# Cross-attention and quantised FFN on one core: setup work, the first and the last step put in another order, and Wo's low part moved to GpSimd

## The reference

```python
y_dca, y_main = y[:, -DCA:, :], y[:, :-DCA, :]
kv_dca = (y_dca @ Wkv_dca + bkv_dca).reshape(b, DCA, 2, H, HD)
k_dca = _ln(kv_dca[:, :, 0], kn_dca_w, kn_dca_b)
v_dca = kv_dca[:, :, 1]
q = _ln((x @ Wq + bq).reshape(b, s1, H, HD), qn_w, qn_b)
k = _ln(kv[..., :HD], kn_w, kn_b)          # kv from y_main @ Wk, y_main @ Wv
ctx = _attn(qT, k, v) + _attn(qT, k_dca, v_dca)
return ctx @ Wo + bo
...
x = x + xattn(_layernorm(x), ctx_1024, ...)
x = x + ffn(_layernorm(x), kernel, bias)   # fake_quant of x, kernel, bias and of relu(...)
```

## Time and profile before

| what | value |
|---|---|
| median of three runs | 357.25 us (355.57, 361.37, 357.25) |
| the profiled execution | 358.21 us, its span 356.4 us |
| PE busy | 326.6 us, 92% of the span |
| DVE busy | 314.6 us, 88% |
| ACT busy | 222.0 us, 62% |
| POOL busy | 173.9 us, 49% |
| shares of the chain that ended last | PE 60%, POOL 8%, DVE 5% |

### The profile page before, as it was taken

One profiled execution on the slowest core, in us unless ns is written; L12 is line 12 of the kernel. 1 busy time (PEld: TensorE's weight loads), 2 busy tenths in 40 slices (PEclk: granted clock), 3 DMA queues, 4 the chain that ended last, 5 costly groups with the idle time before them and its releaser, 6 DMA issues.

```text
span 356.4 us, 7623 instructions
## 1 busy us (share of the span) xinstructions
PE 326.6 (92%) x2372; PEld 257.8 (72%) x2372; DVE 314.6 (88%) x804; ACT 222.0 (62%) x444; POOL 173.9 (49%) x261
## 2 busy tenths in 40 slices
PE   6697879899999999999999999999999999987871
PEld 2354657778888878787878787878787878775640
DVE  2997998889989999999999999999999999986665
ACT  3357986356585858585858585858585856472401
POOL 6211613317282828282828383837373747372720
PEclk9999998699999999999999999999999999999895
DMA  7970334304241514242424242333333323230002
GB/s 259 272 286 3 103 111 151 115 14 136 49 148 48 175 50 149 76 159 67 151 76 147 77 137 90 125 103 118 109 120 106 121 63 120 63 125 25 30 1 88
DMA packets 36451, 38.88 MB, mean 109 GB/s; under 512 B 8760, under 2 KB 27452, under 8 KB 36412
## 3 DMA queue, kind: packets, MB, share of 16 engines
q1 hardware_dynamic: 36044, 38.14, 33.0%
q10 hardware_dynamic: 368, 0.27, 0.3%
HBM read 16.89 MB, written 4.72 MB: 61 GB/s over the span
## 4 chain that ended last, share of the span: by engine, by line
PE 60%; POOL 8%; DVE 5%; issue 4%; ACT 2%; DMA 1%; POOLq 0%; ACTq 0%; DVEq 0%
PE bank L1330 33%; PE bank L1453 9%; POOL finals L536 5%; PE bank L1433 3%; PE bank L1627 3%; PE bank L1434 3%; PE bank L1422 2%; PE bank L1617 2%; PE bank L1474 2%; PE bank L1507 2%; PE bank L1512 1%; POOL x_small L593 1%; DVE seg_out L1075 1%; ACT prob_store L750 1%; DVE rden L1069 1%
## 5 line engine op out<-in xcount | busy, mean ns | idle before, releaser
L517 POOL TENSOR_TENSOR k_lo<-wkv_raw,k_hi 128x448 f16<-128x448 f32 x16 | 16.8, 1047 | 110.5 <-issue 92.9
L1453 PE MATMUL bank<-v_aug,prob_store 128*128 128x66 f32 x512 | 67.9, 276 | 2.7 <-ACT prob_store L750 2.7
L1453 PEld LDWEIGHTS bank<-v_aug,prob_store 128*128 128x128 f32 x512 | 63.7, 193 | 5.2 <-ACT prob_store L750 4.0
L761 ACT ACTIVATE wkv_raw<-bank,affine 128x448 f32<-128x448 f32 (+1 forms) x32 | 22.6, 749 | 40.6 <-PE bank L1507 40.2
L1062 DVE TENSOR_REDUCE neg_max<-bank 128x4 f32<-128x448 f32 (+1 forms) x128 | 44.9, 412 | 0.3 <-PE bank L1422 0.3
L750 ACT ACTIVATE prob_store<-bank,exp_scale 128x512 f32<-128x512 f32 x64 | 41.6, 678 | 4.9 <-PE bank L1434 4.8
L536 POOL TENSOR_TENSOR finals<-seg_out 128x128 f32<-128x128 f32 x64 | 34.5, 547 | 12.5 <-DVE seg_out L1075 11.9
L1433 PE MATMUL bank<-q_stack,k_stack 128*128 128x128 f16 x256 | 33.9, 220 | 0.6 <-ACT maxT L612 0.6
L1434 PE MATMUL bank<-maxT,sel 128*128 128x128 bf16 x256 | 33.7, 219 | 0.0
L1075 DVE TENSOR_TENSOR seg_out<-bank,rden 128x256 f32<-128x256 f32 x64 | 27.2, 424 | 4.0 <-POOL finals L536 1.7
L1433 PEld LDWEIGHTS bank<-q_stack,k_stack 128*128 128x128 f16 x256 | 26.4, 104 | 5.2 <-issue 3.9
(11 more groups left out here) (213 smaller groups left out, 893.7 us busy)
## 6 DMA issues: line engine op xcount, KB each, us to landing
x_in<-in_x SPq DMA_DIRECT2D x16, 256.0 KB, 3.2
q_stack<-q_hi SPq DMA_DIRECT2D x32, 128.0 KB, 2.1
q_stack<-q_lo SPq DMA_DIRECT2D x32, 128.0 KB, 2.1
k_stack<-k_hi SPq DMA_DIRECT2D x32, 128.0 KB, 2.1
k_stack<-k_lo SPq DMA_DIRECT2D x32, 128.0 KB, 2.1
out<-finals SPq DMA_DIRECT2D x16, 256.0 KB, 2.0
y_dcaT<-in_x SPq DMA_DIRECT2D x8, 256.0 KB, 2.9
x_res<-in_x SPq DMA_DIRECT2D x8, 256.0 KB, 2.8
```

The source lines that it names most:

```text
L761: s.activation(n.rearrange("p (c n) -> p c n", n=P)[:, :, 0:keys], src, ACT.Identity, bias=shift, scale=gain).then_inc(n_ready.sem, 1)
L1453: last = mm(bank[6 + gr % 2][:, VW * h:VW * (h + 1)], probs[:, gr % 2, h], v_aug[:, Bt.parity, HG * gr + h], start=True, stop=True)
```

## The change

It has seven parts, none of which changes what is computed. (1) ScalarE copies the selectors in step -2, before the high part of Wq. (2) In step -2 VectorE adds the keys' bias (`biased_keys`) before `setup_norms`, and ScalarE squares the queries before `setup_heads` and `setup_columns`. (3) VectorE works on `setup_ffn(0)` before `low_query` in step 0. (4) `low_output` goes from VectorE to GpSimd, in four pieces of 512 columns between the DCA columns and k's low part of step 0. (5) `setup_ffn_bias` goes from the start of step 0 to the end of step 1, behind the sums of squares and ahead of the maxima. (6) Step 0 on TensorE gets the order of the other steps. (7) In the step where the last batch is Bt, TensorE makes three products of 512 columns (`turn_over`) behind `weigh(2)`, whose result nobody reads.

```diff
+            def low_output():
+                pool.wait_ge(wohi_ready.sem, 1)
+                for c in range(XC):
+                    ins = g.tensor_tensor(wo_lo[:, c], wo_raw[:, c], wo_hi[:, c].bitcast(FP32), ALU.subtract)
+                ins.then_inc(wolo_ready.sem, 1)
@@ pool, step @@
                         dca_columns(k_lo, kdca_lo)
+                        if N.second():
+                            low_output()
                         low(k_lo, k_n, k_hi, kn_ready, khi_ready, kstack_in, klo_ready, MAIN)
@@ scalar @@
                 setup_transposed()
+                setup_selectors()
                 for half in range(2):
@@ scalar, step @@
                         token_statistics()
+                        squared_queries()
+                        setup_heads()
                         setup_columns()
-                        setup_heads()
...
-                if A is not None:
-                    act.wait_ge(*qraw_ready.of(A))
-                    if A.has(1):
-                        act.wait_ge(*qss_ready.of(A.back(1)))
-                    s.activation(q_sq, q_raw[:, A.parity], ACT.Square).then_inc(qsq_ready.sem, 1)
+                if A is not None and not A.first():
+                    squared_queries()
                 if N is not None and N.first():
                     heads(A)
                     setup_wo()
                     setup_values()
                     setup_ffn()
-                    setup_selectors()
@@ vector @@
-            def low_output():
-                dve.wait_ge(wohi_ready.sem, 1)
-                v.tensor_tensor(wo_lo[:], wo_raw[:], wo_hi[:].bitcast(FP32), ALU.subtract).then_inc(wolo_ready.sem, 1)
@@ vector, step @@
-                if Bt is not None and Bt.first():
-                    setup_ffn_bias()
...
                     if A.first():
                         low_queries()
+                        biased_keys()
                         setup_norms()
                         setup_affine()
-                        biased_keys()
                         setup_squares()
                 if Bt is not None and Bt.first():
+                    setup_ffn(0)
                     low_query()
-                    low_output()
-                    setup_ffn(0)
...
                         head_products(A)
+                    if C is not None and C.first():
+                        setup_ffn_bias()
                     maxima(0)
                     maxima(1)
@@ tensor, step @@
-                if Bt is not None and not Bt.first():
+                if Bt is not None:
                     transposed_maxima()
...
-                if Bt is not None and Bt.first():
-                    transposed_maxima()
-                if Bt is not None and not Bt.first():
+                if Bt is not None:
                     first_shifted()
...
-                if Bt is not None and Bt.first():
-                    first_shifted()
...
                     weigh(2)
+                    if final(Bt):
+                        turn_over(bank[3], 3)
```

15 lines of the change are left out of this document (10 added, 5 removed).

## The result

The changed kernel takes 355.26 us (median of 20 runs, 353.64 to 358.64), the kernel before 358.02 us (20 runs beside it). The ratio is 0.9941, with a 95% interval of 0.9918 to 0.9964: 0.6% faster, 2.1 us by the ratio and 2.8 us by the medians, where 6.7 us were forecast. That is clear of noise, but less than the 2% that the prediction sets as its line. The profiled executions are 4.15 us apart, 358.21 and 354.06 us.

The account below looks back on a forecast made before the run. TensorE was taken to bound the later steps, with time to be had in step 0. Terms -8.5 (to step 0's end), +0.1, 0, +1.8 (bias), -0.1 sum to -6.7 us, 358.2 to 351.5, range 348.0 to 356.0.

Parts of the forecast that it names:

- Part 2 and part 1: Steps -2 to 0: earlier queries' square gains 1.7 us, moved selectors' copy 1.9; head of step 0 at 47.9.
- the early 1.7 do not arrive: Rival for step -1: x's transposes or a transfer end last there, so the time is 353.2 us; chance 0.18.
- the 8.5 us: Gain up to the end of step 0, from 72.1 to 63.5, of which 3.6 us came before its head.
- The sum for step 0 (15.6): Step 0's new length in us: TensorE's floor 13.9, plus waits of 0.8 for maxima and 0.9 for context.
- The floor of 13.9: TensorE's work in step 0: a full step's 17.8 us without the Wo and FFN products and four small transposes.
- The transposed maxima, a wait of 0.8: Step 0: TensorE finishes transposes, scores and Wk at about 51.1 and waits 0.8 us for maxima at 51.9.
- The context's wait of 0.9: End of step 0: without an FFN product to fill the time, TensorE waits about 0.9 us for GpSimd's last sum.
- GpSimd's four pieces. Taken: 0: Step 0: pieces of 1.27 us each, 5.1 in all, delay nothing; loss taken 0, ends 0 and 1 us.
- I count no lower clock in it: Step 0: no lower clock in its new length; gain there 8.5 us, or 5.3 if the clock stays as before.
- The first rival, the clock: Steps 0 or 1: the clock falls after TensorE's waits, costing 1.75 to 3.25 us; time 353.2 to 354.8; chance 0.25.
- Step 1 at +0.1: Step 1 loses 0.1 us because VectorE no longer has a lead into it, where `setup_ffn(1)` stands.
- The bias sets a slower rhythm: Rival: late VectorE could cost the 14 steps behind 0.6 us more each, 8.4 in all; time 359.9; chance 0.07.

Follow-up runs that it names:

- a1: The changed kernel with Wo's low part back on VectorE in one instruction behind q's low part (part 4 undone): 354.69 us, ratio 0.9942.
- a2: The changed kernel with the FFN bias back at the start of step 0 (part 5 undone): 355.84 us, ratio 0.9992.
- a3: The changed kernel with GpSimd's four pieces behind `x_plus` instead of ahead of k's low part: 355.23 us, ratio 0.9963.
- c1: The changed kernel with the bias's reduction and two small instructions behind `q_lo` in step 0, its two scalings on GpSimd in step 1: 353.22 us, ratio 0.9875.
- b6: The kernel before with part 1 alone, the selectors copied in step -2: 354.06 us, ratio 0.9896.
- f1: c1 with GpSimd reordered in step 0: `k_lo` after `q_lo`, pieces between the sums, layer norm behind `combine(3)`, `x_plus` last: 352.18 us, ratio 0.9873.
- f3: The changed kernel itself, unaltered, run again on one chip with f4: 354.72 us, ratio 0.9947 to the kernel before.
- g2: The changed kernel with only the bias moved, all five instructions on VectorE behind `q_lo` in step 0: 352.85 us, ratio 0.9871.
- f4: The changed kernel without parts 4 and 5, the same code as d3, run beside f3 on one chip: 353.47 us, ratio 0.9889.
- b5: The kernel before with part 4 alone, Wo's low part in four pieces on GpSimd: 356.48 us, ratio 0.9961.
- d3: The changed kernel without parts 4 and 5: Wo's part on VectorE behind `q_lo`, bias at the start of step 0: 352.81 us, ratio 0.9861.
- a4: The changed kernel with GpSimd's four pieces of 512 columns as one instruction of 2048: 356.37 us, ratio 0.9989.

## Why the prediction was right or wrong

By the profiled execution 4.15 us of 6.7 came. The 2.55 that did not are the head of step 0, 0.9 later than forecast, step 0 itself, 1.55 longer, and the bias, 0.4 dearer, less 0.35 for a shorter step 1. In order of the prediction's steps:

- **Part 2 and part 1: right in kind.** The wait for the selectors went, VectorE's idle 1.89 too (q's square at 29.43), and Wk of step -1 came at 37.2 (forecast 36.5; 36.1 to 36.3 in a1, a2, a3 and c1). The head was at 48.82 instead of 47.9. Of these 0.9 some 0.7 stand already behind the arrival of the weights in step -2, ahead of anything changed: the head of the changed kernel's relatives varies from 47.7 to 49.3. The rival "the early 1.7 do not arrive" is wrong. But the price of part 1 was taken as its wait alone; b6 measured 3.7 us by the ratio, the rest of it by a clock that falls less often. The prediction had that gain within the 8.5 us, under the new order of step 0; b6 has it with the one moved copy. And the 8.5 were read from a profile in which the clock fell twice; the fastest runs of the kernel before (those at a mean clock of 0.986 and more took 354.7 to 356.2 us) had little of that to give back.
- **The sum for step 0 (15.6): wrong, 17.16.** Three terms. The floor of 13.9 was 0.6 too low: TensorE is busy for 14.48 us. "The transposed maxima, a wait of 0.8" was 1.85: `yT_lo` (+0.68), the first (+0.29) and the second half of `max_parts` (+0.78) waited for GpSimd, and 1.05 of this reached TensorE. The context's wait of 0.9 was right (0.84, at 64.09). `weigh(0)` came 9.3 us behind the head, where 7.9 was forecast. f1, with GpSimd out of the way, has 7.86 there, a wait of 0.62 for the maxima and a step 0 of 15.88.
- **"GpSimd's four pieces. Taken: 0": the failed step.** The contention was weighed and its upper end of 1 us is near what it cost in place, 1.05 on TensorE's wait (1.2 against the undisturbed 0.62). The choice of 0 rested on the row for Wv. What ran beside it on VectorE was a reduction (2.28 us from 15.42), and in no run was a reduction held. I had not looked. The pieces did not take 1.27 (5.1 in all) but 6.28. And the pieces are only half of it: a1 without them still had 1.45, since `k_lo`, no longer late behind a lower clock, meets the maxima. The prediction itself had `k_lo` free to start at 51.4 and the maxima at 51.5 to 51.9, and drew nothing from it. I looked for what waits for GpSimd, and not for what GpSimd's instruction holds up. The rows of before had it: `wo_lo` took 3.38 us there from 57.52, beside GpSimd's `x_plus` of 1.74 from 57.0, and 2.28 in a1.
- **"I count no lower clock in it": half wrong.** Right for the profile on which the sum is checked, wrong for others of the same kernel (f3: 1.5 us). The first rival, the clock, put at 353.2 to 354.8 and 0.25, describes a good part of the runs; the median lies 1.2 us above the profiled execution.
- **Part 5: right in kind, +1.8 forecast, +2.2 found**, just above its upper bound of 2.1. The mis-sized term: one scaling took 0.93 instead of 0.49 beside GpSimd's product (83.03 + 1.29). What the forecast lacked was the comparison: a place in step 0, behind `q_lo`, where no cost of it shows (g2).
- **Step 1 at +0.1:** it was 0.25 shorter, since in before a lower clock reached into it. **Part 7 at -0.1:** no difference shows, which fits.
- **"The bias sets a slower rhythm": wrong.** Every step behind step 2 has the same length as before.
- **The new order on TensorE (part 6)** was the centre of the sum and is worth nothing that shows: b6 in the old order has 17.83, f4 in the new 17.96; b5 in the old order with GpSimd's pieces 17.16, as the changed kernel (from a head held by the selectors). The old order hid the wait for the maxima; the prediction saw that ("which the old order hid") and still credited the rest. Part 6 was never run alone, nor the old order with GpSimd out of VectorE's way, so whether f1's 15.88 needs the new order is open.

In sum, by the ratios: part 1 alone gives 3.7 us, part 2 1.3 (0.1 to 2.5), and parts 4 and 5 take some 2 back, in the traces all of it by part 5. The version that beats both kernels is the changed one with the bias behind `q_lo` (g2, 0.9871); c1, d3 and f1 are as fast within their intervals. The kernel before with parts 1, 2 and 4 only was not run. Open: why the clock falls in some executions and not in others behind the same wait.

The rule behind the contention is stated by the Trainium skill (SBUF — State Buffer, Who interferes with whom): the shared port pair is taken for the whole instruction by whoever comes first, and the other blocks; on VectorE's side instructions with two inputs in SBUF, and casts and tensor-scalar operations in a two-port mode, are liable. The traces agree: 3.08 us for `yT_lo` in a4, and a cast (0.47) and scalings (1.51) held too, while `xT_lo`, whose input is in PSUM, kept 0.68 to 0.72 in every run of the table. The contention that the prediction cited I had taken for a slowing in proportion.

## What to carry to other kernels

When work goes to GpSimd, list what VectorE does beside it in that window, not what waits for GpSimd: each two-input instruction (and each scaling or cast between SBUF tensors) there can be held for one whole GpSimd instruction, however small it is itself, so put it where VectorE reads PSUM, and cut it fine. A short TensorE wait can cost more than itself by the clock: one moved copy was worth 3.7 us with a wait of 1.94. One profile can't price that: read the granted clock in each before comparing the lengths of a step. And before moving setup work to a later step, try each place in the same step: ahead of the third exponential the bias's 2.1 us had no cost that shows.

## What was not expected of the hardware

- VectorE's small instructions wait out GpSimd's: 0.19 us became 0.97 to 1.02, 0.38 became 3.08.
- It goes both ways. Of the changed kernel's four pieces (ns least, median, most) the first, beside VectorE's scaling of keys and queries, is the longest:

```profile
L497 POOL TENSOR_TENSOR wo_lo<-wo_raw,wo_hi x4: 1277/1362/2398, 46.7 to 51.7; 128x512 fp32r<-128x512 f32 x4
```

- On GpSimd a tensor-scalar of 512 columns that multiplies and adds took 0.69 us, one that subtracts and multiplies 2.0 (c1, at 64.03) to 3.85 (f1, partly held).
- Waits of 0.7 to 1.9 us were followed by 3.4 us at 1.2 GHz in one execution and by none in another of the same code. Such stretches also stood in step -1 of b5 and b6, where the kernel before had none.
